# Delta attention: upper heads first, the output product behind group 1, the last token products ahead of group 2's state, and fourteen periods in a trip of the loop

## The reference

```
q, k, v = xn @ Wq.T, xn @ Wk.T, xn @ Wv.T
alpha, aR = sigmoid(xn @ Wa.T + ba), sigmoid(xn @ WaR.T + baR)
beta, gamma = sigmoid(xn @ Wb.T + bb), sigmoid(xn @ Wg.T + bg)
def step(carry, inp):
    S, R = carry
    kn = k_t / jnp.maximum(jnp.linalg.norm(k_t, axis=-1, keepdims=True), 1e-12)
    pred = jnp.einsum('bhji,bhj->bhi', S, kn)
    r = jnp.clip(v_t - pred, -CLIP, CLIP)
    S = a_t[..., None] * S
    kp = jnp.einsum('bhd,bhde->bhe', kn, S)
    S = S + b_t[..., None, None] * kn[..., None] * (v_t - kp)[..., None, :]
    o = jnp.einsum('bhji,bhj->bhi', S, q_t)
    ...
return os @ Wo.T + residual
```

## Time and profile before

| | us |
|---|---|
| timed runs (3) | 4647.89, 4661.21, 4664.32; median 4661.21 |
| profiled execution | 4656.47 |
| its span | 4654.8 |
| TensorE busy | 3642.7 (78%) |
| VectorE busy | 2810.7 (60%) |
| ScalarE busy | 1540.1 (33%) |
| GpSimd busy | 887.0 (19%) |

### The profile page before, as it was taken

The page is one execution under the profiler, slowest core; times in us unless marked ns, Lnnn a source line. Parts: engine busy times, 40 slices in busy tenths (PEclk is TensorE's granted clock), DMA queues, the critical chain, the costliest instruction groups (busy, mean ns, idle before and its releaser), DMA issues. The chain is left out here.

```text
span 4654.8 us, 152442 instructions
## 1 busy us (share of the span) xinstructions
PE 3642.7 (78%) x61880; PEld 2596.6 (56%) x61880; DVE 2810.7 (60%) x6331; ACT 1540.1 (33%) x3478; POOL 887.0 (19%) x969
## 2 busy tenths in 40 slices
PE   5777349999958887888888788888878888864877
PEld 4433236766636566566656556656656666642555
DVE  2566452222246776776676776676677677648887
ACT  3222111111124343444344344444344344421111
POOL 1000061111112212212222222321221221210000
PEclk9888659999968998998898998888899989886998
DMA  1000442222120000000000000000000000001000
GB/s 48 21 25 19 152 164 33 34 34 34 28 75 9 7 6 11 7 6 11 7 6 11 7 6 8 9 6 7 10 7 7 10 7 6 6 8 33 21 24 13
DMA packets 90021, 109.39 MB, mean 24 GB/s; under 512 B 14624, under 2 KB 82848, under 8 KB 89248
## 3 DMA queue, kind: packets, MB, share of 16 engines
q1 hardware_dynamic: 58912, 55.39, 4.1%
q0 software_dynamic: 19824, 23.03, 3.4%
q10 hardware_dynamic: 10576, 20.97, 1.3%
HBM read 63.48 MB, written 40.05 MB: 22 GB/s over the span
## 5 line engine op out<-in xcount | busy, mean ns | idle before, releaser
L1209 ACT COPY da_Ub<-da_U 32x256 f32<-32x256 f32 x1024 | 412.0, 402 | 45.0 <-ACT da_U L1202 7.2
L903 POOL TENSOR_TENSOR da_M<-da_M,da_decay 128x512 f32<-128x512 f32 x256 | 278.3, 1117 | 755.0 <-DVE da_prev_end L1018 402.8
L1043 DVE TENSOR_TENSOR da_eGn<-da_eGn,da_z 128x30 f32<-128x30 f32 (+14 forms) x960 | 352.5, 367 | 32.9
L1042 DVE TENSOR_TENSOR da_z<-da_eGn 128x30 f32<-128x30 f32 (+14 forms) x960 | 348.4, 363 | 29.0 <-DVE da_eGn L1043 1.6
L1490 PE MATMUL da_C<-da_Ub,da_Km 128*64 128x256 f32 x2048 | 307.5, 417 | 22.2 <-DVE da_M L1066 10.0
L1388 PE MATMUL da_unit<-da_cum,da_sp 128*128 128x132 f32 x1024 | 206.1, 372 | 111.4 <-DVE da_ssm L997 78.8
L1329 PE MATMUL da_unit<-da_xnT,da_wx 128*128 128x128 f32 x2048 | 265.8, 293 | 10.2 <-ACT da_eGn L1194 9.0
L1322 PE MATMUL da_unit<-da_wx,da_xnT 128*128 128x512 f32 x512 | 254.1, 621 | 23.5 <-ACT da_xnT L1155 21.9
L676 PE MATMUL moe_ps_up<-moe_up,moe_zsT 128*128 x568 | 270.1, 599 | 1.4 <-ACT moe_zsT L595 1.4
L1329 PEld LDWEIGHTS da_unit<-da_xnT,da_wx 128*128 128x128 f32 x2048 | 257.8, 208 | 18.8 <-issue 15.2
L694 PE MATMUL moe_ps_dn<-moe_down,moe_hT 128*128 x1136 | 257.0, 379 | 0.6 <-DVE moe_hT L554 0.6
(11 more groups left out here) (290 smaller groups left out, 7603.1 us busy)
## 6 DMA issues: line engine op xcount, KB each, us to landing
moe_zs<-moe_slots SPq DMA_DIRECT2D x71, 129.0 KB, 2.1
la_x<-in_x SPq DMA_DIRECT2D x64, 128.0 KB, 2.0
moe_up<-in_upT ACTq DMA_DIRECT2D x8, 1024.0 KB, 13.9
moe_down<-in_downT ACTq DMA_DIRECT2D x8, 1024.0 KB, 12.8
stream<-la_y SPq DMA_DIRECT2D x32, 128.0 KB, 1.7
moe_x<-stream SPq DMA_DIRECT2D x8, 512.0 KB, 5.4
da_x<-moe_acc SPq DMA_DIRECT2D x128, 32.0 KB, 1.9
stream<-da_xz SPq DMA_DIRECT2D x128, 32.0 KB, 1.5
```

The lines of the kernel that those rows point to most:

```text
L903: ins = nc.gpsimd.tensor_tensor(st_, st_, decay[:, par, rec, 2 * g:2 * g + 2].rearrange("p a b -> p (a b)").unsqueeze(2).to_broadcast([P, ...
L1042: c.link(tt(t, Xm[:, s + 1:C, s:s + 1].to_broadcast([P, below, s]), Xm[:, s:s + 1, 0:s].to_broadcast([P, below, s]), ALU.mult))
L1043: c.link(tt(Xm[:, s + 1:C, 0:s], Xm[:, s + 1:C, 0:s], t, ALU.add))
L1209: ins = nc.scalar.copy(Ub[rows_of(b), :, :, b, :], U[rows_of(b), rec])
```

## The change

Ten periods more are written out in a trip of the loop (UN goes from 4 to 14, so 28 periods are 2 trips and no longer 7). The keys and queries of the upper half of the heads go first, and the products of a half wait for that half only. In the first part of a period queries and turned keys stand behind the first solve, and the norms of the keys ahead of the first state update. The output product stands behind group 1's second solve and waits for the eviction of group 3's gram. The last two grams stand ahead of group 2's work on TensorE. On VectorE group 2's clipping stands behind four pairs of the substitution, and the later pieces stand behind more of them. On ScalarE the logarithms of the rates come last in the period. The order of GpSimd and SyncE within a period is as it was.

```diff
-        GROWN = ((0, 1, 2), (1, 2, 0))
+        GROWN = ((1, 2, 0), (1, 2, 0))
...
-        UN = 4
+        UN = 14
...
             def products(n, par, rec, half):
...
-                need(dve, g_ready, n * 6 + ((2, 3), (6, 5))[rec][half])
-                need(dve, q_ready, n * 2 + 2)
+                need(dve, g_ready, n * 6 + ((3, 2), (6, 5))[rec][half])
...
+                need(dve, k_ready, n * 2 + 2 - half)
...
+                need(dve, q_ready, n * 2 + 2 - half)
+                tt(tokens(F[:, :, 2 - rec, :]), up[:, :, :, 1:PL], query, ALU.mult).then_inc(prod_ready, 1)
...
                 if state:
                     clipped(i, par, 0)
+                if prepare:
+                    norms_of_keys(n)
+                if state:
                     update(i, 0, 0)
+                if prepare:
+                    gates(n)
...
                 if prepare:
                     products(n, pn, 0, 0)
+                    gram_out(n, pn, 3)
                     products(n, pn, 1, 0)
                 if state:
                     state_rows(i, 2)
-                    update(i, 1, 1)
-                if prepare:
-                    gram_out(n, pn, 3)
+                if prepare:
                     decays(pn, 0)
                     decays(pn, 1)
+                if state:
+                    update(i, 1, 1)
+                if prepare:
                     gram_out(n, pn, 0)
-                if state:
-                    clipped(i, par, 2)
-                if prepare:
                     gram_out(n, pn, 1)
                     triangle_in(n, pn)
+                    substitute(1, 5)
+                if state:
+                    clipped(i, par, 2)
+                if prepare:
+                    substitute(5, 8)
                 if state:
                     update(i, 2, 0)
                 if prepare:
-                    substitute(1, 6)
+                    substitute(8, 11)
                 if state:
                     state_rows(i, 3)
                     update(i, 2, 1)
                 if prepare:
-                    substitute(6, 11)
+                    substitute(11, 15)
                 if state:
                     clipped(i, par, 3)
...
-                    substitute(11, 14)
+                    substitute(15, 18)
...
-                    substitute(14, 20)
+                    substitute(18, 22)
...
-                    substitute(20, C - 1)
+                    substitute(22, C - 1)
                     triangle_out(n)
...
                 if norm:
                     rate_exp(i + 2, 3)
-                    rate_log(i + 2)
                 if prepare:
                     turned_keys(n, 1)
                     values(n, 1)
                 if state:
                     outputs(i, 3)
                 if prepare:
                     turned_keys(n, 2)
+                if norm:
+                    rate_log(i + 2)
...
             def result(i):
                 need(pe, oT_ready, (i + 1) * NG)
-                if exists(i + 1):
+                if exists(i + 2):
+                    need(pe, gram_done, once(i + 2, 1))
+                elif exists(i + 1):
                     need(pe, km_ready, once(i + 1, 3))
...
                 if prepare:
                     for part in GROWN[0]:
                         growth(n, 0, part)
+                    keys(n, pn, 1)
+                    keys(n, pn, 0)
                 if put:
                     turned_outputs(i - 1, 3)
                 if prepare:
-                    keys(n, pn, 0)
-                    keys(n, pn, 1)
-                if state:
-                    turned_keys(i, 3)
-                if prepare:
-                    queries(n, pn, 0)
                     queries(n, pn, 1)
                 if state:
                     solve(i, 0, 0)
                     state_outputs(i, par, 0)
                 if prepare:
+                    queries(n, pn, 0)
+                if state:
+                    turned_keys(i, 3)
+                    inner_predicted(i, par, 0)
+                if prepare:
                     norms_of_keys(n)
-                if put:
-                    result(i - 1)
-                if state:
-                    inner_predicted(i, par, 0)
+                if state:
                     state_update(i, 0, 0)
...
                 if state:
                     solve(i, 1, 1)
                     inner_outputs(i, par, 1, 0)
-                    turned_outputs(i, 0)
+                if put:
+                    result(i - 1)
+                if state:
                     inner_outputs(i, par, 1, 1)
                     state_rows(i, par, 2)
                     state_update(i, 1, 1)
+                if prepare:
+                    gram(n, pn, 0)
+                    gram(n, pn, 1)
+                if state:
+                    turned_outputs(i, 0)
                     state_predicted(i, par, 2)
                     solve(i, 2, 0)
                     state_outputs(i, par, 2)
-                if prepare:
-                    gram(n, pn, 0)
-                if state:
+                    turned_outputs(i, 1)
                     inner_predicted(i, par, 2)
-                if prepare:
-                    gram(n, pn, 1)
-                if state:
                     state_update(i, 2, 0)
...
```

More of the change, by code:

```diff
@@ L1168, in keys @@
                 need(act, decay_ready, n)
-                need(act, k_psum, n * 2 + half + 1)
+                need(act, k_psum, n * 2 + 2 - half)
                 bank = un[:, 1 + half]
@@ L1175, in queries @@
             def queries(n, half):
-                need(act, q_psum, n * 2 + half + 1)
+                need(act, q_psum, n * 2 + 2 - half)
                 nc.scalar.copy(QT[:, half * HB:(half + 1) * HB], un[:, 1 + half].rearrange("p (h t) -> p h t", t=P)).then_inc(q_ready, 1)
@@ L1231, in period @@
                         growth(n, 0, part)
+                    keys(n, 1)
+                    keys(n, 0)
                 if put:
@@ L1234, in period @@
                 if prepare:
-                    keys(n, 0)
-                    keys(n, 1)
+                    queries(n, 1)
+                if state:
+                    solved(i, 0, 0)
+                if prepare:
+                    queries(n, 0)
                 if state:
@@ L1250, in period @@
                 if state:
-                    solved(i, 0, 1)
+                    outputs(i, 0)
+                    solved(i, 1, 0)
                 if prepare:
@@ L1265, in period @@
                 if state:
-                    outputs(i, 2)
-                if prepare:
-                    values(n, 0)
-                if state:
                     turned_outputs(i, 2)
+                    solved(i, 3, 0)
                 if norm:
                     copy_xT(i + 2, par)
-                if state:
-                    solved(i, 3, 0)
-                if norm:
                     for u in range(3):
@@ L1332, in keys @@
             def keys(n, par, half):
-                need(pe, g_ready, n * 6 + 2 + half)
+                need(pe, g_ready, n * 6 + 1 + half)
                 turned(un[:, 1 + half], par, 2, half).then_inc(k_psum, 1)
             def queries(n, par, half):
-                need(pe, k_ready, n * 2 + half + 1)
+                need(pe, k_ready, n * 2 + 2 - half)
                 turned(un[:, 1 + half], par, 3, half).then_inc(q_psum, 1)
@@ L1362, in norms_of_keys @@
             def norms_of_keys(n):
-                need(pe, q_ready, n * 2 + 1)
+                need(pe, q_ready, n * 2 + 2)
                 need(pe, k_ready, n * 2 + 2)
@@ L1418, in turned_keys @@
                     if exists(n + 1):
-                        need(pe, g_ready, (n + 1) * 6 + 1)
+                        need(pe, g_ready, (n + 1) * 6 + 3)
                 elif exists(n + 1):
@@ L1551, in period @@
                     gates(n, pn)
-                    growth(n, 1, 1)
-                    growth(n, 1, 2)
                 if state:
@@ L1557, in period @@
                 if prepare:
-                    growth(n, 1, 0)
+                    growth(n, 1, 1)
+                    growth(n, 1, 2)
                 if state:
@@ L1566, in period @@
                 if prepare:
+                    growth(n, 1, 0)
                     gram(n, pn, 2)
```

72 lines of the change are left out of this document (32 added, 40 removed).

## The result

The changed kernel takes 4809 us in the median (4795 to 4818) against 4655 (4647 to 4664) for the one before: a ratio of 1.033, with a 95% interval of 1.029 to 1.036. The forecast of 4625 was wrong by 184 us and on the wrong side. The profiled execution has 4812.0 us and a span of 4810.3.

A forecast was written before the change was run, and what follows sets the result against it. TensorE and VectorE were taken to form a ring, no single engine the bound. Stretches of 50.85 and 36.25 us made a period 87.1 against 87.49, -12 us in all; with -20 for jumps, 4656.5 became 4625, range 4530 to 4712.

The forecast's parts named there:

- The queue: GpSimd's output issues wait for the output's copy, ahead of scaled values and factors; takes 3.7 us a period back.
- first stretch: From growth's first product to VectorE's triangle, 57.8 us, called TensorE's; forecast to end at 50.85.
- Sum 9.2, so gram 2 starts at 27.2: On TensorE, output product, waits and lower clock no longer ahead of group 2's gram: 9.2 us off its 36.4 start.
- worked example: One period taken from the timeline, 87.49 us, from which the forecast took its lengths.
- the 0.9 us credited for the lower clock behind the norms' wait: On TensorE, two groups of 32 products at 1.08 against 0.65 later; gives 0.9 us more.
- Second stretch: From VectorE's triangle to the next growth, 29.7 us before; forecast to grow to 36.25.
- Contention with GpSimd: Rescalings of groups 3, 0 and 1 beside VectorE's triangle and first pairs cost 1.5 us a period, bounds 0 to 3.9.
- The jumps: Jumps back in the loop pause TensorE's growth about 4.0 us each; five fewer save 20 us, bounds 0 and 21.5.
- Rival 4: The jumps' pauses do not go, since longer straight code pauses elsewhere: 4645 us; chance 0.05.
- Rival 2: Slower: TensorE's clock falls in new idle time before group 2's second solve; period 90.5, time 4723; chance 0.20.
- Rival 1: GpSimd doesn't bind; TensorE stops the period at 83.5 us, time 4520; chance 0.20.
- Rival 3: A wash in the period, 87.5 us, and only the jumps count: 4636 us; chance 0.15.

The follow-up runs named there:

- vn_first: Changed kernel with only group 2's scaled values ahead of the output's DMA issues in GpSimd's queue: 4782 us, ratio 1.030.
- out_last: Changed kernel with the output's four DMA issues at the very end of GpSimd's period: 4616 us, ratio 0.9944.
- log: out_last with ScalarE's first logarithm of the rates ahead of the last copy of turned keys: 4569 us, ratio 0.9854.
- before_un14: Kernel before with fourteen periods in a trip instead of four, nothing else: 4616 us, ratio 0.9952.
- filled: Changed kernel with 14 unused products added on TensorE in its wait between grams 0 and 1: 4811 us, ratio 1.035.
- back: Changed kernel with the output product, its copy and their waits in their old places, GpSimd's order untouched: 4578 us, ratio 0.988.
- out_mid: Changed kernel with the output's four DMA issues behind the scaled values of groups 2 and 3 and the factors on GpSimd: ratio 1.0055.

## Why the prediction was wrong

**The queue was seen and sized about right.** Forecast: from the output's copy to the triangle 10.05 us, of which the queue costs 3.7. Measured: 10.3, and the queue costs 4.2, by the triangle at 55.1 and at 50.9 with the queue cleared. (The forecast counts to `ncT`, the table here to the operation behind it, 0.15 us later.) It named the factors as releaser, but these are there at 53.9 and the chain over the scaled values ends 0.9 us later; with group 2's values taken out of it (vn_first) the factors do release the triangle, 1.4 us earlier. It had the values at about 4.2 behind the copy, measured 4.7, and gave the work behind them on VectorE no term. Both chains wait for the same issues. Measured on the whole kernel, the queue costs 127 us, and with the rescaling that it pushes beside the triangle 178. That is more than the entire loss of 155.

**The step that failed is the sum of the first stretch: "Sum 9.2, so gram 2 starts at 27.2".** Over the 27 periods gram 2 starts at 30.6, which is 5.3 before the old mean of 35.9. All times behind it are as late: output product 39.7 for a forecast 36.2, end of its copy 44.8 for 40.8, triangle 50.9 for 47.1 without the queue. Of the 9.2 credited 5.3 came. Four causes of the missing 3.9 can be read from the traces, of 1.0, 0.6, 0.6 and about 1.5 us; no run tried them one by one. The output product was taken at 5.3 from a worked example in which it ran at the lower clock for 3.4 us; in the kernel before it has 136.9 us in 32 periods, 4.3 each, and in its new place the forecast itself charged it only 4.1. The wait for the norms went, but 0.6 us of waiting for VectorE remain ahead of group 0's second solve. The products of the keys now wait 1.3 us for growth's exponentials (L1336, 34.6 us in 27), where the kernel before waited 0.7 for them, ahead of the turned outputs and of the keys:

```profile
PE da_unit L1513 <- ACT da_eGn L1194: 13.2, 24, 1.3
...
PE da_unit L1329 <- ACT da_eGn L1194: 6.3, 18, 0.4
```

And the 0.9 us credited for the lower clock behind the norms' wait weren't gained. The clock fell elsewhere: gates, solve and growth (2333.4 to 2338.7 in the period above) ran at the lower level: the second solve takes 1.07, the first 0.65. Ahead of gram 2 TensorE stands at the lower level for 10.5 us a period where it was 9.1, and at 1.07 for 0.65 that costs some 0.6 us (an estimate) on top of the 0.9.

**Second stretch: forecast 36.25, measured 38.6.** Without GpSimd beside it, 36.4 for a forecast of 34.75. The worked example isn't to blame: its 29.7 is the old mean of 30.8 less the jumps' pauses, 1.0 a period. From the triangle to the last addition of the rates (L986) out_last takes 28.7 us and the kernel before 21.6, so 7.1 more where the forecast had 5.95 (clipping, four pairs and the clock). Ahead of the first of these additions VectorE now waits 1.7 us a period for TensorE, 0.96 for inner predictions and 0.76 for state updates, where it waited 0.2 before; the forecast had 0.7 for TensorE there, as clock. From the last addition to growth it takes 7.7 us instead of 8.2 without the pauses: of the -0.9 for ScalarE's new order about half came, since the last copy of turned keys stands ahead of the table load with its wait; log took that back and more.

Contention with GpSimd was put at 1.5 and measures 2.2. That is inside its bounds of 0 to 3.9. The Trainium skill (SBUF — State Buffer, "SBUF: two separate sides") describes an exclusive lock, held for a whole instruction, between GpSimd and those VectorE operations that have two inputs in SBUF. The trace agrees in the rows of the period above: L1034 runs in 1.26 us and the rescaling beside it takes 2.0 instead of 1.0, and then the last two of the six rescalings end at 2372.69 and 2373.69 and the two first operations of the substitution right behind them, at 2372.74 and 2373.76, the latter after 0.73 and 0.99 us instead of 0.20 and 0.21. The prediction drew from it a price near its upper end, and that didn't come: 7.03 us of rescaling cost 2.2, since few operations of this kind (mainly L1034, L1041, L1042) meet it before it is over.

**The jumps** were right: forecast 20, measured 22 in the kernel before (15 to 29). One pause is left in the changed kernel, 4.1 us at 2783.70. Rival 4 is out. The pauses in dense rows are another matter: the prediction set them down to the fetching of straight code, and no run ties them to it. With as many instructions, the inner prediction has 31.0 us of them before, 21.8 in before_un14 and 8.0 in the changed kernel.

**Rival 2** (slower, 4723) had the sign, but not by its mechanism. It put the price on TensorE's clock ahead of group 2's second solve. That wait is there (L1467, 88.7 us in 42), and so is the lower clock (652 us of the 27 periods, 450 before), but what filled gained by the clock right ahead of it was lost again, while the queue's two lines took the whole loss away. Rival 1 foresaw what an unbound GpSimd would be worth, 4520, and out_last took 4616: the first stretch was too long for it. Rival 3, no change in the period, is out by 5 us.

**In sum.** 87.1 was forecast and 93.65 measured, 6.55 apart: 3.8 in the first stretch without the queue, 0.5 in the queue, 1.6 in the second stretch without GpSimd, 0.7 in GpSimd's share. Times 29 periods that is about the 187 us between 4624.5 and 4812. The part outside GpSimd's share, 5.4, came from the output product's length and the clock's credit, 2.5 together, and for most of the rest from crediting each wait removed to an order whose own new waits were not sought, on TensorE in the first stretch and on VectorE in the second. The worked example, 87.49, is a fair one as a whole (88.5 less 1.0 of pauses); what it had wrong was the length of one row, the output product. Of the 93.65, 0.6 are the two long periods at the jump.

The range (4530 to 4712) failed with it. Both marks set for a wrong forecast were crossed: triangle above 53 and second stretch above 38.5.

What stays open: back is faster than the kernel before with fourteen periods by 1.1 us a period by the ratios (0.988 against 0.9952), and how much of it comes from the upper heads' order and how much from the token products was not tried apart. Nor was the place of group 2's clipping and of the later pieces in the substitution, behind which VectorE's new waits stand.

## What to carry to other kernels

When a step moves, ask of every engine it issues to what stands behind it in that engine's queue; an issue that must wait belongs at the end of an in-order queue, behind all that could run without it. Moving two lines there was worth 178 us, more than the whole change had lost. Take the lengths in a sum from means over many periods, and only their order from a worked example. And before crediting a wait that goes, look in the new order for what now waits in its place: when the longest wait was removed alone (vn_first), 231.6 us of waiting went and some 15 us of time.

## What the runs showed of the hardware

VectorE's operations with two inputs in SBUF suffer beside GpSimd's, but its transposition, with one, does not: the 128x1024 product L1034 takes 1.73 us in the changed kernel's mean and 1.22 in back's, the 128x1024 transposition L1033 1.93 and 1.90.

```profile
L1033 DVE STREAM_TRANSPOSE da_eGn<-da_gm 128x1024 f32<-128x1024 f32 x32 | 61.6, 1926 | 0.0
L1034 DVE TENSOR_TENSOR da_eGn<-da_eGn,da_ncT 128x1024 f32<-128x1024 f32 x32 | 55.5, 1733 | 1.1
```

7 us of rescaling cost 2.2 us of the stretch here. In out_last the last 4 us of it (47.0 to 51.0 into the period) end as the triangle starts, at 50.9, and the first stretch is no longer for that than out_mid's.

Products put into a wait of TensorE raised its granted clock (0.87 to 0.89 over the 27 periods), and did not make the kernel faster. Where a wait on TensorE's own path was shortened, ahead of growth, 42 us came instead of 29, with 1.7 us a period less at the lower clock behind it.
